# Hidden rows of both directions without a gap: 96 lanes instead of 112 in DRAM and in the projection's buffers

## What is computed

```python
def step(carry, xr):                        # one image row: (B=8, 48, W=96)
    h, c = carry
    inp = jnp.concatenate([xr, h], axis=1)
    gates = conv1d_3taps(inp, w_mid) + b
    i, f, g, o = jnp.split(gates, 4, axis=1)
    c2 = sigmoid(f) * c + sigmoid(i) * tanh(g)
    h2 = sigmoid(o) * tanh(c2)
    return ((h2, c2), h2)
hs_f = scan(step, rows, reverse=False)      # H=96 steps
hs_b = scan(step, rows, reverse=True)
feats = jnp.concatenate([hs_f, hs_b], axis=2)        # 96 channels
y = jnp.einsum('oc,bchw->bohw', w_proj, feats)       # 48 <- 96 channels
x = relu(batch_norm(y)) + x                          # mean, var over all pixels
# then: mask, top-k choice of 144 of 288 hidden channels,
# 1x1 conv 48 -> 288, depthwise 3x3, 1x1 conv 288 -> 48, + x
```

## Time and profile before

| | us |
|---|---|
| median of 3 runs | 1936.3 (1934.2 to 1939.63) |
| the profiled execution | 1932.55 |
| its span in the trace | 1930.7 |
| recurrence, to the last h | 984.9 |
| from there to the first product of the projection | 10.6 |
| projection, first product to last | 128.6 |
| from the last product's start to the residual's first instruction | 3.3 |
| residual | 74 |
| selection, gather, bottleneck | 729 |

### The profile page before, as it was taken

The page is one execution under the profiler, slowest core; times in us unless marked ns, Lnnn a source line. Parts: engine busy times, 40 slices in busy tenths (PEclk is TensorE's granted clock), DMA queues, the critical chain, the costliest instruction groups (busy, mean ns, idle before and its releaser), DMA issues. The chain is left out here.

```text
span 1930.7 us, 43828 instructions
## 1 busy us (share of the span) xinstructions
PE 1690.1 (88%) x16464; PEld 1259.7 (65%) x16464; DVE 1443.7 (75%) x2308; ACT 1321.3 (68%) x2395; POOL 17.0 (1%) x37
## 2 busy tenths in 40 slices
PE   5999999999999999999955520779999999999997
PEld 5999999999999999999941100543333333333333
DVE  5777777777777777777743466558988888888897
ACT  5888888888888888888843345036555555565564
POOL 2000000000000000000000000000000000000000
PEclk9999999999999999999979975579999999999999
DMA  4555555555555555555559988001111111111111
GB/s 115 149 143 144 142 140 146 149 142 145 142 140 146 149 142 144 143 140 146 141 149 249 253 177 205 2 16 44 58 44 51 51 58 44 58 58 54 49 58 59
DMA packets 84517, 221.32 MB, mean 115 GB/s; under 512 B 19796, under 2 KB 21208, under 8 KB 84440
## 3 DMA queue, kind: packets, MB, share of 16 engines
q1 hardware_dynamic: 82260, 212.69, 40.9%
q10 hardware_dynamic: 2180, 7.57, 1.8%
HBM read 96.43 MB, written 49.55 MB: 76 GB/s over the span
## 5 line engine op out<-in xcount | busy, mean ns | idle before, releaser
L264 PE MATMUL gates<-state,w_high 64*128 64x384 f32 x4608 | 505.0, 337 | 0.0
L1367 DVE SCALAR_TENSOR_TENSOR acc<-h1d,wt,acc 128x768 f32<-128x768 f32 x480 | 484.0, 1017 | 24.5 <-ACT acc L1257 12.4
L264 PEld LDWEIGHTS gates<-state,w_high 64*128 64x128 f32 x4608 | 417.1, 185 | 0.0
L1106 PE MATMUL psd<-h1p,wt 64*64 64x384 f32 x3456 | 300.9, 487 | 6.0 <-ACT h2p L1289 6.0
L264 PE MATMUL gates<-state,w_low 64*128 64x384 f32 x2304 | 268.1, 338 | 0.0
L264 PE MATMUL gates<-x_both,w_high 64*128 64x384 f32 x2304 | 237.4, 338 | 18.8 <-DVE w_low L380 18.8
L1106 PEld LDWEIGHTS psd<-h1p,wt 64*64 64x64 f32 x3456 | 124.3, 132 | 180.9 <-issue 173.6
L264 PEld LDWEIGHTS gates<-x_both,w_high 64*128 64x128 f32 x2304 | 207.6, 186 | 18.7 <-issue 18.7
L317 ACT ACTIVATE sig_f<-gates 48x384 f32<-48x384 f32 x384 | 187.3, 488 | 37.2 <-PE gates L264 32.1
L264 PEld LDWEIGHTS gates<-state,w_low 64*128 64x128 f32 x2304 | 209.2, 185 | 0.0
L411 DVE TENSOR_TENSOR h_new<-sig_o,tanh_c 128x384 f32<-128x384 f32 x192 | 107.2, 558 | 122.3 <-ACT tanh_c L335 122.3
(11 more groups left out here) (136 smaller groups left out, 1773.3 us busy)
## 6 DMA issues: line engine op xcount, KB each, us to landing
x_taps<-x_both SPq DMA_DIRECT2D x192, 195.5 KB, 3.1
x_raw<-x_steps SPq DMA_DIRECT2D x192, 192.0 KB, 3.1
h_in<-h_rows SPq DMA_DIRECT2D x48, 672.0 KB, 6.5
x_last<-x_both SPq DMA_DIRECT2D x192, 98.0 KB, 2.9
h_rows<-h_new SPq DMA_DIRECT2D x96, 192.0 KB, 2.9
base<-y SPq DMA_DIRECT2D x48, 336.0 KB, 3.1
out<-base SPq DMA_DIRECT2D x48, 336.0 KB, 2.7
h_rows<-h_new SPq DMA_DIRECT2D x96, 144.0 KB, 2.6
```

Source lines behind the costliest of these rows:

```text
L264: return nc.tensor.matmul(gates[p][d][:, m, 0:NH], w[own, n, m, :], moving[own], start=start, stop=stop)
L1106: mm = nc.tensor.matmul(psd[64 * m:64 * m + 64, i, 0:NH], wt[own, to:to + 64], h1[own, dy + 4 * m:dy + 4 * m + 4, dx:dx + W], start=(tap = ...
L1367: nc.vector.scalar_tensor_tensor(a, window(h1d[d % 2], tap), par(D_UNITS[s], TAP + tap), a, ALU.mult, ALU.add).then_inc(acc_done if tap == ...
```

## The change

`h_rows` gets 96 lanes instead of 112: lanes 0 to 47 for the forward direction, 48 to 95 for the backward one. Both stores take 48 lanes. The projection's buffers and weights have 96 lanes, each load fills all of them (96 x 1536 float32, 576 KB), and the products contract over 96 lanes. The clearing of the buffers and the three waits for it go. `wp` is loaded with two transfers of 48 lanes, which skip the zero lanes of the input `w_proj`, and TensorE waits for both.

```diff
@@ recurrence, store_h
-                    own = slice(HI * d, HI * d + (HI if d == 0 else HC))
-                    sp.dma_start(h_rows[two, own, e if d == 0 else 1 - e], h_new[e][own]).then_inc(h_stored[e], 16)
+                    sp.dma_start(h_rows[two, HC * d:HC * d + HC, e if d == 0 else 1 - e],
+                                 h_new[e][HI * d:HI * d + HC]).then_inc(h_stored[e], 16)
@@ projection
-        wp = ctx.enter_context(nc.sbuf_tensor("wp", [P, 64], F32))
-        h_in = [ctx.enter_context(nc.sbuf_tensor(f"h_in{n}", [P, ROWS, B, W], F32)) for n in range(BUFS)]
+        wp = ctx.enter_context(nc.sbuf_tensor("wp", [2 * HC, 64], F32))
+        h_in = [ctx.enter_context(nc.sbuf_tensor(f"h_in{n}", [2 * HC, ROWS, B, W], F32)) for n in range(BUFS)]
...
-            sp.dma_start(wp[:], w_proj).then_inc(wp_loaded, 16)
+            for d in range(2):
+                sp.dma_start(wp[HC * d:HC * d + HC], w_proj[HI * d:HI * d + HC]).then_inc(wp_loaded, 16)
...
-                    if first:
-
-                        sp.wait_ge(gaps_zero, n + 1)
...
-                    sp.dma_start(h_in[n][0:HI + HC], h_rows[BUFS * i + n]).then_inc(h_loaded[n], 16)
+                    sp.dma_start(h_in[n][:], h_rows[BUFS * i + n]).then_inc(h_loaded[n], 16)
...
-            pe.wait_ge(wp_loaded, 16)
+            pe.wait_ge(wp_loaded, 32)
...
-            for n in range(BUFS):
-                nc.vector.memset(h_in[n][96:128], 0.0).then_inc(gaps_zero, 1)
@@ build
-    h_rows = nc.dram_tensor("h_rows", [H // 2, HI + HC, 2, B, W], F32).ap()
+    h_rows = nc.dram_tensor("h_rows", [H // 2, 2 * HC, 2, B, W], F32).ap()
```

More of the change, by code:

```diff
@@ L448, in sem @@
             return ctx.enter_context(nc.semaphore(name))
-        wp = ctx.enter_context(nc.sbuf_tensor("wp", [P, 64], F32))
-        h_in = [ctx.enter_context(nc.sbuf_tensor(f"h_in{n}", [P, ROWS, B, W], F32)) for n in range(BUFS)]
+        wp = ctx.enter_context(nc.sbuf_tensor("wp", [2 * HC, 64], F32))
+        h_in = [ctx.enter_context(nc.sbuf_tensor(f"h_in{n}", [2 * HC, ROWS, B, W], F32)) for n in range(BUFS)]
         ps = ctx.enter_context(nc.psum_tensor("proj", [P, TURN, 512], F32))
-        wp_loaded, gaps_zero = sem("wp_loaded"), sem("gaps_zero")
+        wp_loaded = sem("wp_loaded")
         h_loaded = [sem(f"h_loaded{n}") for n in range(BUFS)]
@@ L459, in _, with body @@
         def _(sp):
-            sp.dma_start(wp[:], w_proj).then_inc(wp_loaded, 16)
-            def body(i, first):
+            for d in range(2):
+                sp.dma_start(wp[HC * d:HC * d + HC], w_proj[HI * d:HI * d + HC]).then_inc(wp_loaded, 16)
+            def body(i):
                 for n in range(BUFS):
-                    if first:
-                        sp.wait_ge(gaps_zero, n + 1)
                     r = TURN * i + ROWS * n
                     at_least(sp, row_summed, r - TURN + ROWS)
-                    sp.dma_start(h_in[n][0:HI + HC], h_rows[BUFS * i + n]).then_inc(h_loaded[n], 16)
-            body(0, True)
+                    sp.dma_start(h_in[n][:], h_rows[BUFS * i + n]).then_inc(h_loaded[n], 16)
+            body(0)
             with sp.Fori(1, H // TURN) as i:
-                body(i, False)
+                body(i)
         @block.tensor
         def _(pe):
-            pe.wait_ge(wp_loaded, 16)
+            pe.wait_ge(wp_loaded, 32)
             def body(i, first):
```

## The result

The changed kernel took 1928.1 us (median of 8 runs, 1924.45 to 1931.53) against 1936.88 us before (8 runs, 1934.2 to 1943.16). The ratio is 0.9952, with a 95% interval from 0.9933 to 0.9970. So it is faster by about 9 us, which is clear of no change, but less than half of the 19.4 us that were forecast. The profiled execution took 1927.23 us with a span of 1925.7.

What follows compares the result with a forecast made beforehand. TensorE was taken to bound the recurrence and the transfer of bytes the projection. Savings of 18.0 + 0.9 + 0.4 + 0.1 = 19.4 us from the median of 1936.3 gave 1916.9 us, range 1910 to 1929.

Steps and rivals of the forecast that it cites:

- the 2.45: Sign of error for the projection: a period per load over 2.45 us would prove the forecast wrong.
- What bounds the kernel: TensorE bounds the recurrence; the transfer of bytes bounds the projection, with DMA engines busy 95.8% of the time.
- The steady state, 18.0 us: Projection's loads: the period falls from 2.736 to 2.345 or 2.362 us with the bytes, saving 18.0 us over 47 periods.
- the sentence on the round trip: Projection's three buffers: a round trip of 6.35 us, 2.12 us per load, stays below the period of 2.35 us.
- The assumption that an engine's time per lane stays: Projection's loads: each engine moves six lanes instead of seven at unchanged time per lane; the 18.0 us rest on it.
- The products, 1.51 us: TensorE in the projection: eight records per load still take 1.51 us over 96 lanes, hidden by the load.
- The start, 0.9 + 0.4 + 0.1 us: Projection's start: first load issued 0.9 us earlier and landing 0.4 us sooner; last stores before it gain 0.1 us.
- Behind it: Residual merely moved, bottleneck's start shifted against the clock's rise: 0 us, at most 2.5 us either way.
- The first, a lower bandwidth of 96 lanes: Rival, projection's loads: 96 lanes get only 234 GB/s, 2.52 us per load, time 1924.8 us; chance 0.12.
- The fourth, TensorE as the bound: Rival, projection's products: a row's two halves no longer run side by side, 2.58 us per load, 1927.6 us; chance 0.03.
- The second: Rival, projection's loads: lanes below 64 set the pace, period stays 2.736 us, time 1934.9 us; chance 0.05.
- the third: Rival, projection's loads: transfers get in each other's way, 197 GB/s, 2.99 us per load, 1947.0 us; chance 0.05.

Runs made afterwards that it cites:

- e1_over128: The changed kernel with its products contracting over 128 lanes again, lanes 96 to 127 cleared, loads still of 96 lanes; 1927.7 us, ratio 0.996 to before.
- e13_96_four: The changed kernel with products over 128 lanes again and four buffers for h instead of three, loads of 96 lanes; 1915.1 us, ratio 0.988 to before.
- e2_only96: The kernel before with only the contraction narrowed to 96 lanes, its loads still of 112 lanes; 1940.5 us, ratio 1.001 to before.
- e16_after_four: The changed kernel, loads and products of 96 lanes, with four buffers for h instead of three; 1916.4 us, ratio 0.990 to before.
- e14_before_four: The kernel before, with loads of 112 lanes, given four buffers for h instead of three; 1936.9 us, ratio 0.999 to before.
- e8_both128: The kernel before with h and the residual's x both loaded in single transfers of 128 lanes, three buffers for h, products over 128; 1902.0 us.
- e6_two48: The kernel before with each load of h as two transfers of 48 lanes, to lanes 0-47 and 64-111, products over 128; 1951.5 us, ratio 1.008.

## Why the prediction was right and wrong

The time, 1928.1 us, lies just inside the range, near the end that had been put there for a lower bandwidth. That is no success of the forecast, 19.4 us from a period of 2.35, which didn't come true. The period was 2.64 us, over the 2.45 at which I had said that I would be wrong.

- **What bounds the kernel.** Right as to the stage: every gain of the runs above lies in the projection or the residual. Wrong in the reading of the limit: "the engines hardly ever lack work" from a share of 95.8%. It was true of the 112 lanes of before (a fourth buffer gave nothing), but the share as such is no proof; e1_over128 and e13_96_four have 101.7% and 101.5%, and 226 and 249 GB/s.
- **The steady state, 18.0 us.** This is the term that failed; it measured 4.6. The step that failed is the sentence on the round trip, "6.35 us over three buffers is 2.12 us per load", with its cover of 0.2 us. It took the time from issue to use of the very first load, alone in the queue, and products at full clock. In the changed kernel a load landed after 5.3 us (median), its products took 2.0 us in the mean (97.0 us for 48 loads), and the period was 2.64. At full clock, in e1_over128, it was 2.605 us, and three of them are 6.0 us to land, 1.51 of products and 0.3 for the hand-overs. That sum alone proves nothing, because the landing time holds whatever a load queues. The fourth buffer does: it took the time from the first product to the last from 122.46 to 110.0 us. So the cover wasn't there, and 0.26 us per load went, 12 us. The assumption that an engine's time per lane stays failed with three buffers (a packet took 0.44 us at full clock, 0.38 before) and holds with four: 2.34 us in e13_96_four, 2.37 in the middle of the stage, where I had 2.345 to 2.362. With full clock and four buffers the whole stage takes 123.3 us, where the forecast had 142.5 - 19.4 = 123.1.
- **The products, 1.51 us.** The record's duration at full clock is 1.51 us per load, as said. I had weighed the lanes only as a price per record and never as something that could change the granted clock, though the prediction itself noted both levels in the trace. Measured against the kernel with the same transfers and 128 lanes in the contraction, that costs 1.5 us in the changed kernel, 6.9 in e2_only96 and 2.3 in e16_after_four.
- **The start, 0.9 + 0.4 + 0.1 us.** The two weight transfers and the first load stand 0.85 us apart (forecast 0.82), which gives 1.74 - 0.85 = 0.89. The first load was used 4.87 us after its issue instead of 5.12, 0.25. From the last store's issue to `wp` it is 3.09 us instead of 3.70, 0.6, of which I had forecast 0.1. In all 1.75 for 1.4.
- **Behind it.** 0.93 us came back. The bottleneck's first product stands at 1267.01 (1274.10 before), and the clock rose only some 13 us later instead of 9, as the windows behind this paragraph show. This lay in the 2.5 us that I had allowed.
- **The rivals.** The first, a lower bandwidth of 96 lanes, gave 1924.8 and describes what came (222 to 226 GB/s in the stage, 1928.1), but as an effect of layout and buffers together. The fourth, TensorE as the bound, came true for part of the time, by the clock and not by the columns. The second and the third didn't occur. The rule cited beside the second does bear on this case, but in another place than I looked, see the last section.

Two windows of the changed kernel around the clock's rise in the bottleneck, against the earlier trace rows:

```profile
1267.00:1280.00 13.00, 9.43 (x32) 2.62 (x36) 1.67 (x2) 5.17 (x11) 0.00 (x0) 0.50 0.11 33
1280.00:1290.00 10.00, 9.40 (x96) 3.83 (x92) 9.68 (x11) 5.84 (x9) 0.00 (x0) 0.97 0.01 2
```

**What stays open.** Why 96 lanes with three buffers settle at 226 GB/s in lanes 0 to 95 and at 240 in lanes 32 to 127, and why e14_before_four gains nothing while e13_96_four gains 0.26 us per load, isn't settled. The runs show that lanes and buffers have a part in it, and that another pitch in DRAM changed nothing. How three buffers make packets of 96 lanes slower while the engines' share stays over 100% is open too. That engines meet at the same lanes is only argued.

## What to carry to other kernels

Fewer bytes in a transfer-bound stage are a gain only if neither the round trip of the buffers nor the rate itself depends on what was cut. Test the first with one more buffer before believing a DMA share near 100%. The landing time doesn't replace this test: that of the first load leaves out what others in flight do to it, and that of later loads holds their queueing. For the second, a load of all 128 lanes with padding moved a third more bytes than one of 96 in the same time with three buffers (2.59 and 2.61 us) and in less with four (2.02 and 2.34). And when a contraction is narrowed while TensorE has pauses, look at its granted clock.

## What the runs showed of the hardware that was not expected

- The rate of transfers with 6144 B runs by their lanes: 48 lanes at a time 170 GB/s (in an execution slower than the other four, whose rate is an estimate of 190), 96 lanes 226 to 249 (at full clock and with TensorE not the bound), 112 lanes 249 to 251, 128 lanes 305 with three buffers, 390 with four, and 415 in the residual of e8_both128. The Trainium skill, "DMA: Bandwidth & Descriptors", section "Rules for kernel authors", asks for one transfer of 128 lanes and warns of two on disjoint halves; the trace agrees: two transfers of 48 lanes reached 170 GB/s where one of 96 reached 226 for the same bytes with three buffers, and 128 lanes reached 305. Of the same skill, "SBUF — State Buffer", section "Door 1: The DMA port swizzle", has lanes 0 to 63 on 8 of 16 ports; by its 27.2 GB/s per port a transfer to one half is an estimate of at most 218 GB/s, and e6_two48, with every transfer in one half, stayed under it.
- A product over 96 or 112 lanes with pauses between loads (clock 0.76 and 0.77) lost the full clock where one over 128 lanes with the same records, of which 32 lanes are zeros, kept it (1.00). With hardly a pause (busy 83.92 of 85 us) 96 lanes kept it too. 128 lanes are no guarantee: e6_two48, whose pauses were the longest (some 2.0 us per load), ended the stage at 0.50.
- The DMA share reaches 101 to 103% in seven of these windows. At that level it didn't tell whether the same loads could go faster: 226 and 249 GB/s stood at 101.7% and 101.5%.
